# Two heads at a time: maxima and exponentials of a pair together, its transposes a step later, one of its copies moved to VectorE

## The reference

```
block 0: linear attention (16 heads) with its own MLP; then a mixture of 8 experts: silu(x Wg) * (x Wu) Wd, summed
block 1: causal attention, 8 heads of 16 channels ("the small attention")
         then the last feed-forward, itself an attention over 16 heads of 64:
         v     = mixture of 8 value projections, the top 2 by a gate
         probs = softmax(q k^T / 8)            # per head, 512 x 512
         attn  = probs v
         res   = sum over heads of (top-2 mask of experts) * attn * Wo
```

## Time and profile before

| what | value |
|---|---|
| median of 3 runs | 2792.04 us (2791.95 to 2797.8) |
| profiled execution, its own time | 2791.24 us |
| its span, first to last instruction | 2789.5 us |
| mean granted TensorE clock | 0.931 |
| copies of prT on ScalarE | 512, 306.4 us in all |
| exponentials of the heads on ScalarE | 512, 351.7 us |
| maxima of the heads on VectorE | 512, 339.8 us |
| transposes of the heads on TensorE | 2048, 293.1 us |

### The profile page before, as it was taken

One profiled execution on the slowest core, in us unless ns is written; L12 is line 12 of the kernel. 1 busy time (PEld: TensorE's weight loads), 2 busy tenths in 40 slices (PEclk: granted clock), 3 DMA queues, 4 the chain that ended last, 5 costly groups with the idle time before them and its releaser, 6 DMA issues.

```text
span 2789.5 us, 41424 instructions
## 1 busy us (share of the span) xinstructions
PE 2402.2 (86%) x15724; PEld 1394.2 (50%) x15724; DVE 1492.0 (53%) x2621; ACT 1392.8 (50%) x2944; POOL 794.4 (28%) x373
## 2 busy tenths in 40 slices
PE   3887698898989898899989989899988998898697
PEld 2343344554456544565446544565445543464465
DVE  4332574456734576346753577345753457337842
ACT  0334344763466634664447634665447642554274
POOL 1000373005800165003720057002650039004600
PEclk7895898999989999999999999999999999998799
DMA  2110020012101130002200221001300031001101
GB/s 82 41 64 1 10 67 1 17 40 74 44 1 31 46 80 16 17 16 76 65 1 16 62 61 35 9 24 54 77 12 16 16 89 46 1 16 33 26 27 39
DMA packets 210689, 101.15 MB, mean 36 GB/s; under 512 B 137367, under 2 KB 189620, under 8 KB 210492
## 3 DMA queue, kind: packets, MB, share of 16 engines
q1 hardware_dynamic: 205052, 95.74, 12.6%
q10 hardware_dynamic: 5440, 2.75, 0.4%
HBM read 77.48 MB, written 20.99 MB: 35 GB/s over the span
## 4 chain that ended last, share of the span: by engine, by line
PE 57%; DVE 9%; issue 8%; ACT 8%; POOL 4%; DMA 1%; ACTq 0%; DVEq 0%; SPq 0%; POOLq 0%
PE bank L822 9%; PE bank L1118 9%; PE bank L1149 8%; PE bank L940 5%; PE bank L943 5%; PE bank L948 4%; POOL prod L807 3%; PE bank L980 3%; ACT pr L1324 2%; PE bank L1130 2%; DVE nmax L1675 2%; ACT prT L1341 2%; PE bank L1040 2%; ACT arena L1245 1%; PE bank L1107 1%
## 5 line engine op out<-in xcount | busy, mean ns | idle before, releaser
L807 POOL TENSOR_TENSOR prod<-pv,mixv 128x1024 f32<-128x1024 f32 x218 | 636.3, 2953 | 155.9 <-DVE vals L1638 119.8
L1675 DVE TENSOR_REDUCE nmax<-bank 128x1 f32<-128x512 f32 x512 | 339.8, 685 | 360.1 <-PE bank L1118 357.0
L1324 ACT ACTIVATE pr<-bank,nmax 128x512 f32<-128x512 f32 x512 | 351.7, 687 | 361.0 <-DVE nmax L1675 358.6
L747 POOL TENSOR_TENSOR rstd<-vareps,minus_half 128x4 f32<-128x4 f32 x48 | 49.4, 1029 | 1478.3 <-DVE vareps L1429 1478.3
L1341 ACT ACTIVATE prT<-bank 128x512 f32<-128x512 f32 x512 | 306.4, 599 | 111.0 <-PE bank L822 94.8
L1222 ACT ACTIVATE arena<-bank 128x512 f32<-128x512 f32 x256 | 152.9, 597 | 412.5 <-PE bank L940 394.6
L1638 DVE TENSOR_REDUCE vals<-prod 128x128 f32<-128x1024 f32 x224 | 269.4, 1210 | 70.7 <-POOL prod L807 70.4
L940 PE MATMUL bank<-h1T,Wg 128*128 128x512 f32 x512 | 272.3, 614 | 37.8 <-ACT prT L1341 19.7
L1557 DVE TENSOR_REDUCE nmax<-bank 128x1 f32<-128x128 f32 (+3 forms) x256 | 113.9, 486 | 356.5 <-PE bank L982 356.3
L822 PE MATMUL bank<-ident,pr 128*128 128x128 f32 x2048 | 293.1, 287 | 10.5 <-ACT prT L1341 5.5
L1149 PEld LDWEIGHTS bank<-prT,vals 128*64 128x64 f32 x3584 | 206.5, 145 | 189.7 <-issue 155.5
(11 more groups left out here) (239 smaller groups left out, 2968.5 us busy)
## 6 DMA issues: line engine op xcount, KB each, us to landing
Wg<-in_L_ffn_Wg SPq DMA_DIRECT2D x64, 256.0 KB, 2.7
Wu<-in_L_ffn_Wu SPq DMA_DIRECT2D x64, 256.0 KB, 3.1
Wd<-in_L_ffn_Wd SPq DMA_DIRECT2D x64, 256.0 KB, 3.6
out_rows<-on SPq DMA_DIRECT2D x32, 512.0 KB, 2.6
onR<-out_rows SPq DMA_DIRECT2D x32, 512.0 KB, 4.1
xin<-in_L_attn_x SPq DMA_DIRECT2D x8, 256.0 KB, 5.5
mask_rows<-masko SPq DMA_DIRECT2D x8, 256.0 KB, 4.4
maskR<-mask_rows SPq DMA_DIRECT2D x8, 256.0 KB, 7.2
```

What stands on the lines that cost most here:

```text
L807: g.tensor_tensor(*value_piece(n), ALU.mult).then_inc(vprod_r[0], 1)
L1324: s.activation(pr[:, x % NPR, :], S[x % len(S)][:, :], ACT.Exp, bias=nmax[:, x % NPR:x % NPR + 1], accum_out=den[:, i % 2, h:h + 1]).then_ ...
L1675: v.tensor_reduce(nmax[:, m % NPR:m % NPR + 1], S[m % len(S)][:, :], X_AXIS, ALU.max, negate=True).then_inc(nmax_r[0], 1)
```

## The change

It does three things to the 64 heads of every batch.

1. VectorE computes the two maxima of a pair in the even head's step, one after the other, and ScalarE the two exponentials. The odd step has neither.
2. The transposes of a pair move from the even step to the odd step after it (`turned_at` now gives a pair in odd steps). They are the same transposes of the same heads, later in TensorE's order by whatever stands between the two steps.
3. In the odd step ScalarE copies only the even head's transposes; VectorE copies the odd head's (`pT_v`). The waits on `pT_r` become waits on the one of the two that counts the head in question, or on both.

```diff
+def pair_at(k, lag):
+
+    m = HEAD_OF[k] - lag
+    return (m - 1, m) if m % 2 and 0 <= m < N2 else ()
+
+
 def turned_at(k):

-    m = HEAD_OF[k] - 2
-    return (m, m + 1) if m % 2 == 0 and 0 <= m < N2 else ()
+    return pair_at(k, 2)
...
-        pT_r = sem("pT_r", N2)
+        pT_r = sem("pT_r", N2 // 2)
+        pT_v = sem("pT_v", N2 // 2)
...
                 if sum(b) >= 2:
-                    wait(pe, pT_r, behind(b, 2), LAST_ODD + 1)
+                    wait(pe, pT_v, behind(b, 2), LAST_ODD // 2 + 1)
...
                 if what == "head":
-                    wait(pe, pT_r, b, n + 1)
+                    wait(pe, (pT_r, pT_v)[n % 2], b, n // 2 + 1)
...
                 if use[0] == "head" and (is_last(b) or not in_tb(use[1])):
-                    wait(pe, pT_r, b, use[1] - 1)
+                    wait(pe, (pT_r, pT_v)[use[1] % 2], b, use[1] // 2)
...
-                        wait(pe, pT_r, b, m + 1)
+                        wait(pe, pT_r, b, m // 2 + 1)
+                        wait(pe, pT_v, b, m // 2 + 1)
...
-                    if kind == "head":
-                        wait(s, nmax_r, b, x + 1)
-                        if x >= NPR:
-                            wait(s, p_T, b, x - NPR + 1)
-                        i, h = x // HS, x % HS
+                    for m in (x, x + 1) if kind == "head" and x % 2 == 0 else ():
+                        wait(s, nmax_r, b, m + 1)
+                        if m >= NPR:
+                            wait(s, p_T, b, m - NPR + 1)
+                        i, h = m // HS, m % HS
...
-                    m = lagging(k, 2)
-                    if m is not None:
+                    for m in turned_at(k)[0:1]:
                         wait(s, p_T, b, m + 1)
                         s.activation(prT[:, m % 3, :], probs_bank(b, m)[:, :], ACT.Copy).then_inc(pT_r[0], 1)
...
-                    if kind == "head":
-                        wait(v, s_ps, b, m + 1)
-                        if m >= NPR:
-                            wait(v, pr_r, b, m - NPR + 1)
...
+                    for n in (m, m + 1) if kind == "head" and m % 2 == 0 else ():
+                        wait(v, s_ps, b, n + 1)
+                        if n >= NPR:
+                            wait(v, pr_r, b, n - NPR + 1)
...
+                    for n in turned_at(k)[1:2]:
+                        wait(v, p_T, b, n + 1)
+                        v.tensor_copy(prT[:, n % 3, :], probs_bank(b, n)[:, :]).then_inc(pT_v[0], 1)
```

More of the change, by code:

```diff
@@ L862, in attn0 @@
                 yield 3
-                for s in (pr_r, xout_r, oa_r, pT_r):
+                for s in (pr_r, xout_r, oa_r, pT_r, pT_v):
                     if sum(b) >= 3:
@@ L1051, in begin @@
                 wait(pe, pT_r, b, 0)
+                wait(pe, pT_v, b, 0)
                 if sum(b) + 2 < NB:
@@ L1316, in steps @@
                         s.activation(qs[:, x % 3, :, :].rearrange("p a t -> p (a t)"), bank_x[:, :], ACT.Copy).then_inc(qs_r[0], 1)
-                    if kind == "head":
-                        wait(s, nmax_r, b, x + 1)
-                        if x >= NPR:
-                            wait(s, p_T, b, x - NPR + 1)
-                        i, h = x // HS, x % HS
+                    for m in (x, x + 1) if kind == "head" and x % 2 == 0 else ():
[3 more added lines that the diff above has]
+                        i, h = m // HS, m % HS
                         if h == 0 and (i >= 2 or i == 0 and is_last(b)):
                             wait(s, rden_r, b, max(0, 2 * (i - 1)))
-                        s.activation(pr[:, x % NPR, :], S[x % len(S)][:, :], ACT.Exp, bias=nmax[:, x % NPR:x % NPR + 1], accum_out=den[:, i % 2, h:h + 1]).then_inc(pr_r[0], 1)
+                        s.activation(pr[:, m % NPR, :], S[m % len(S)][:, :], ACT.Exp, bias=nmax[:, m % NPR:m % NPR + 1], accum_out=den[:, i % 2, h:h + 1]).then_inc(pr_r[0], 1)
                     if kind == "mixed":
@@ L1670, in steps @@
                         v.tensor_tensor(on[:, half, :], bank_x[:, :].rearrange("p (h d) -> p h d", d=DS), rden[:, m % 2, :].unsqueeze(2).to_broadcast([P, HS // 2, DS]), ALU.mult).then_inc(on_r[0], 1)
-                    if kind == "head":
-                        wait(v, s_ps, b, m + 1)
-                        if m >= NPR:
-                            wait(v, pr_r, b, m - NPR + 1)
-                        v.tensor_reduce(nmax[:, m % NPR:m % NPR + 1], S[m % len(S)][:, :], X_AXIS, ALU.max, negate=True).then_inc(nmax_r[0], 1)
+                    for n in (m, m + 1) if kind == "head" and m % 2 == 0 else ():
+                        wait(v, s_ps, b, n + 1)
+                        if n >= NPR:
+                            wait(v, pr_r, b, n - NPR + 1)
+                        v.tensor_reduce(nmax[:, n % NPR:n % NPR + 1], S[n % len(S)][:, :], X_AXIS, ALU.max, negate=True).then_inc(nmax_r[0], 1)
+                    for n in turned_at(k)[1:2]:
+                        wait(v, p_T, b, n + 1)
+                        v.tensor_copy(prT[:, n % 3, :], probs_bank(b, n)[:, :]).then_inc(pT_v[0], 1)
                     if k in BUILD_AT:
```

## The result

The changed kernel takes 2731.43 us (median of 4 runs, 2726.63 to 2734.99) against 2794.92 us before (4 runs, 2791.95 to 2800.89): ratio 0.9769, 95% interval 0.9742 to 0.9796. The forecast was 2746 us, range 2705 to 2790. The profiled execution took 2734.99 us, its span is 2733.2 us.

A forecast was written before the change was run, and what follows sets the result against it. TensorE, busy 86% of the span, was taken as the bound. Six stages at -6.55 us gave -39.3, with batch 6 and the last pass -45.8: 2745.4 from the profiled 2791.24, forecast 2746 us, range 2705 to 2790.

The forecast's parts named there:

- (a): Score pairs in each stage: with maxima and exponentials adjacent, pairs no longer split; -5.4 us a stage, bounds 0 and -7.1.
- (b): Small attention's loop: moved head transposes cover TensorE's waits on ScalarE; -3.5 us a stage, bounds 0 and -14.9.
- (c): Extras (queries, back, mixed, result matmuls) wait for the TB copy behind two exponentials; +3.1 us a stage, bounds 0 and +14.
- The last rival, the wait on TB: Extras in the stages exposed at the bound, 14 us a stage instead of 3.9: slower, 2817 us; chance 0.13.
- (d): Start of the experts: both maxima come first and VectorE copies head 61; -0.75 us a stage, bounds 0 and -3.27.
- (e): Batch 6: gains about 5.0 us, pays 1.5 for extras and 3.5 for tail copies on VectorE; sum 0, bounds -9, +6.
- (f): Last pass: VectorE's copy starts as soon as transposes end, removing prT waits; -6.5 us, bounds 0 and -7.2.
- The clock rival: Stages: fewer gaps give back half the loss to the lower clock, 36 us more over six stages: 2710 us; chance 0.17.

The follow-up runs named there:

- M: Part 1, a pair's maxima and exponentials together in the even step: the changed kernel without it 2757.13 us; of the change only it 2760.03 us.
- T: Part 2, a pair's transposes in the odd step: the changed kernel without it 2774.81 us; of the change only it 2781.5 us.
- V: Part 3, VectorE copying the odd head's transposes: the changed kernel without it, ScalarE making both copies, 2713.09 us; never run alone.
- the run with six heads of room: Changed kernel with the odd half's back step one head earlier, mixed and result one later, six heads between back and mixed instead of four: 2701.34 us.

## Why the prediction was right, step by step

The direction was right and the stages carry it; the size was too small, -45.8 us forecast and -63.5 measured between the medians (-56.3 between the profiled spans). That it came so near is in part luck: the stages gave 12.9 us more than forecast and batch 6 9.9 more, the last pass 6.3 less, and the front, where nothing changed, took 8.7 longer in the profiled execution. The terms by themselves:

**(a) Split pairs: right, a little too large.** At full clock all pairs of a stage but three run in one block, from the first to the last matmul's start 0.54 us; at heads 34, 50 and 56 it is 0.81, where it was 1.52, 1.87 and 1.88. Taking M out costs 4.2 us a stage (201.3 against 197.1), with what the extras then wait more; I had 5.4.

**(b) The loop: right in mechanism, too small.** -3.5 us a stage forecast, -6.5 of waits measured, and -3.4 of clock that I had left to a rival. TensorE's two waits fell from 104.0 to 59.3 us, by 43%, where I had said a fifth. The runs give it by parts: at full clock the loop is about 83 before, 80.9 with M, 78.4 with T, 78.9 with M and T, 76.4 with T and V, 76.5 with all three. So T carries it, V adds 2.0 to 2.4 that I had not priced apart, and M adds nothing once T is there. My account by places may also have counted the first cover of each wait and not that the next place starts earlier as well; no run shows that by itself.

**(c) The extras: right in kind, too small.** Waits on prT ahead of extras rose by 41.5 us (16.5 to 58.0), 25 forecast. Behind the loop at full clock the stage did not get shorter at all (36.6 + 58.7 before, 36.4 + 58.9 after), while the pairs there and the start of the experts should have given some 5 us; that much the extras and VectorE's copy take back. VectorE's copy is about 1.6 of it (35.2 + 58.5 without it), so the extras are some 3 to 4 us in time, against the 3.1 that I wrote. The place that I took as the pattern, with the start of the experts behind it:

```profile
950.29 1.29 DVE L1682 TENSOR_REDUCE nmax<-bank 128x1 f32<-128x512 f32 x2 [2.07 <-PE bank L1125]
...
952.36 0.59 ACT L1348 ACTIVATE prT<-bank 128x512 f32<-128x512 f32 x1
952.62 0.68 DVE L1685 COPY prT<-bank 128x512 f32<-128x512 f32 x1
...
953.00 0.66 PE L1129 MATMUL bank<-ident,oaT 128*128 128x128 f32 x4 [0.70 <-ACT prT L1348]
...
958.34 0.68 DVE L1685 COPY prT<-bank 128x512 f32<-128x512 f32 x1
...
959.08 1.34 PE L946 MATMUL bank<-h1T,Wg 128*128 128x512 f32 x2 [2.31 <-DVE prT L1685]
```

The extra waits 0.70 us where it waited 0.25, the +0.45 that the step worked out as +0.5. The number of exposed extras was right as well: 7 of the 19 wait in each stage, 5 or 6 before, and I counted eight. What was too low is the size at the other places: the seven wait 7.5 us together, 2.57 of it at the result of batch 1, where 0.50 stood before.

```profile
939.95 3.15 DVE L1443 TENSOR_SCALAR nrm_o<-h_odd,mv,rstd 128x128 f32<-128x128 f32 x4
...
943.02 1.27 DVE L1682 TENSOR_REDUCE nmax<-bank 128x1 f32<-128x512 f32 x2
...
945.99 1.91 PE L1143 MATMUL bank<-WoG,ymT 128*128 128x128 f32 x8 [2.57 <-ACT prT L1348]
```

There the pair's maxima start only when the norms on VectorE end, and two exponentials and a copy of oaT stand between them and the copy, which starts at 945.33. The step took its pattern from a place where VectorE is idle for 2.07 us ahead of the maxima. That the two exponentials are not all of it is shown by the exchanged copies: with the even head's copy on VectorE the extras still wait 51.1 us. The last rival, the wait on TB, thus came true in kind and not in size.

**(d) Into the experts: right in size, half right in cause.** 3.27 to 2.31 us at this place, -0.97 on the mean of six waits (19.7 to 13.9 us), -0.75 forecast. But with M and T alone the six waits are 14.7 us already; VectorE's copy, which the step names, adds 0.13 each.

**(e) Batch 6: the step that failed.** Sum 0 forecast, -9.9 measured, as a difference of three misjudged parts. The loop there fell by 15.8 us where I gave it 3.5; some 7 of them are clock (17 us at half clock before, none after). Behind the gates the pairing is worth 7.9 us (102.7 to 94.8 with M alone) where I gave (a) some 1.5: the pairs of heads 48, 52 and 56 took 4.9, 5.5 and 4.2 us there from their first to their last start, and before the change TensorE's largest wait in that stretch was

```profile
PE bank L1118 <- ACT pr L1324: 12.5, 5, 3.4
```

And the copies cost 10.3 us where I took 3.5 and bounded it at 5.4. I had priced eight copies at their own length, and the run moved ten; TensorE also waits 3.7 us for `on`, 2.3 for `xout` (2.5 before) and 3.3 for VectorE's copies there, all gone in the run with the tail on ScalarE, and its half-clock time is 36.2 us against 24.4 in that run.

**(f) The last pass: the wait went as said, the time didn't.** The 6.4 us of prT waits are gone, and the pass is 120.7 us where 114 was forecast. The earlier trace rows leaves out a row between its two that shows the next wait, at the mixed matmuls, before the change:

```profile
PE bank L1130 <- issue: 1.8, 3, 1.1
```

The same wait of the changed kernel in the pass (beside it only 0.8 us for an exponential), then the timeline of one round trip:

```profile
PE bank L1137 <- issue: 5.6, 3, 2.9
```

```profile
2621.60 0.60 PE L1129 MATMUL bank<-ident,oaT 128*128 128x128 f32 x4
...
2623.36 0.33 SPq L687 DMA_DIRECT2D out_rows<-on  x1
...
2625.98 0.37 SPq L689 DMA_DIRECT2D onR<-out_rows  x1
...
2631.01 2.06 PE L1137 MATMUL bank<-spread,onR 128*64 128x32 f32 x64 [1.70 <-issue]
```

Back to mixed takes 9.4 us here, and the four heads between them are 7.7 us of TensorE's work, the 9.4 less the wait. The profile calls this wait "issue"; that it is the transfer is shown by the landing of `onR`, 4.94 us after its issue at 2625.98, 0.1 us ahead of the mixed matmuls, and by the run with six heads of room, where the wait is gone. The other 3 us are the half-clock piece at 2693.8 us, busy 6.42 of 6.90 us at 0.51. The sum closes: less its waits and 0.4 of its half-clock time the pass is 111 to 112 us before (120.9 less 9.0), after (120.7 less 6.4 and 2.7), with the extras later (115.2 less 3.7) and with room (112.9 less 0.7 and 1.1). The step that failed: a wait that goes was taken as time that goes, without asking what is late next.

**The clock rival** came true in the loops and not in the kernel: half-clock time in the whole span went from 386 to 410 us. The Trainium skill ("TensorE: Matmul & The Clock Gate", Part 1) says that the clock follows how busy the engine has lately been. The loop's rows agree (busy 72.17 of 84.70 at a mean of 0.98, 70.48 of 76.60 at 1.00), and so does a new low stretch further on: at 945.99 us TensorE has waited 2.57 us for ScalarE's prT copy, and 946.2 to 949.6 us is granted 0.50. The total that I gave for this rival was 2710.

**The copy on VectorE.** The Trainium skill ("TensorEngine Tiling (Array Packing)", PSUM Bottleneck) advises both engines for emptying PSUM. By the trace that holds in part: beside M and T the copy loses 14.3 us from the first heads on (2270.7 without it, 2285.0 with it; the medians are 2713.09 and 2731.43) and gains 2.4 us in each loop. It paid in the loop, where VectorE is busy 39.66 of 76.60 us, and cost at the end of batch 6, where it is busy 61.93 of 65. In the last pass, busy 70.25 of 121, no gain shows (119.4 us without it, 120.7 with it), so room on the second engine was not enough by itself.

## What to carry to other kernels

Take a change of several moves apart and price each in each stage: here two moves gave 31 and 9 us alone and 88 together (40, 22 and 80 by the trace), and the third paid only beside one loop. Where a wait is removed, follow the next dependence back to its start, transfers included, because an unnamed "issue" wait ahead of a step that reads a DMA's rows can be the new bound. A pattern place prices a step only where the engines are as free as there: look at the worst place too. And an engine at 58 of 62 us may not take a copy at its own length: ask what stands queued behind it.

## What the runs showed of the hardware

The stretch ahead of the first heads has the same instructions in all these kernels, and its length differs by up to 12 us between the profiled executions: 437.7 us with 143 us at the lower clock level, 439.4 with 147, 443.3 with 159, 449.8 with 174. The windows of the kernel without V and of the changed kernel:

```profile
0.00:437.70 437.70, 327.71 (x1100) 162.02 (x1100) 201.47 (x476) 138.34 (x224) 118.75 (x89) 0.84 0.15 42
```

```profile
0.00:448.10 448.10, 337.38 (x1100) 168.24 (x1100) 201.55 (x476) 138.36 (x224) 118.64 (x89) 0.80 0.14 41
```

Same counts, same VectorE and ScalarE time; only TensorE's busy time and granted clock differ. That is 0.4% of the kernel, more than several of the terms above, so stages were compared with stages and not by totals alone. From the first heads on the change gains 65.1 us (2350.1 to 2285.0). Here each us more at the lower level goes with 0.3 to 0.4 us of length (12.1 for 31 between the first and the last of the four, 10.4 for 35 between the two windows), close to the 0.4 of the loops.
